# Writing out the sixteen token-group steps of an attention-and-experts kernel, and placing weight preparation, filler products and the hand-over to its second phase anew

## The reference: what is computed

```python
xn = layernorm(x)
x = x + attn(xn) + ffn(xn)
# attn: 16 heads of 8; scores = cov(q, k)/8 + var(q)*var(k)/8, softmax, times v, times Wo
# ffn:  transformer block on xn. Its attention runs over the 32 SEQUENCES (causal),
#       for each of the 256 positions; x1 = xn + that; then layernorm, a router over 8 experts,
#       the top 2 of them: gates * gelu(h @ w1[e]) @ w2[e]; returns x1 + y
```

## Time and profile before

| | |
|---|---|
| runs | 1037.51, 1038.67, 1039.70 us; median 1038.67 |
| profiled execution: time, span | 1042.3 us, 1040.6 us |
| groups, up to the last `causal_pv` | 0 to 337 us |
| lead-in | 337 to 392.5 us |
| expert blocks | 392.5 to 541 us |
| sequence steps | 541 to 1040.6 us |
| busy: PE, DVE, ACT, POOL | 87%, 77%, 66%, 59% of the span |

### The profile page before, as it was taken

The page is one execution under the profiler, slowest core; times in us unless marked ns, Lnnn a source line. Parts: engine busy times, 40 slices in busy tenths (PEclk is TensorE's granted clock), DMA queues, the critical chain, the costliest instruction groups (busy, mean ns, idle before and its releaser), DMA issues.

```text
span 1040.6 us, 34011 instructions
## 1 busy us (share of the span) xinstructions
PE 902.4 (87%) x11962; PEld 564.5 (54%) x11962; DVE 805.8 (77%) x2168; ACT 688.4 (66%) x1395; POOL 619.2 (59%) x886
## 2 busy tenths in 40 slices
PE   3687787888787458999998999999999999999997
PEld 2464554555555325788874555555555555555543
DVE  5878687789888374555566899999999999999880
ACT  3667677778886213443445778778777877787774
POOL 4146475676666662222225777877877777787751
PEclk9678899899999657999997999999999999999998
DMA  6515622122221133777741111111111111111111
GB/s 161 78 32 102 151 67 56 49 68 56 52 64 43 41 112 106 227 224 225 232 139 26 39 44 52 36 49 44 49 39 43 50 37 48 44 49 39 41 47 31
DMA packets 110824, 80.52 MB, mean 77 GB/s; under 512 B 23296, under 2 KB 97920, under 8 KB 110720
## 3 DMA queue, kind: packets, MB, share of 16 engines
q1 hardware_dynamic: 99328, 51.78, 20.3%
q0 software_dynamic: 11392, 27.35, 8.6%
HBM read 44.83 MB, written 33.73 MB: 75 GB/s over the span
## 4 chain that ended last, share of the span: by engine, by line
PE 43%; POOL 19%; issue 14%; DVE 13%; ACT 10%; POOLq 0%; DVEq 0%; DMA 0%; ACTq 0%
PE bank L712 36%; POOL xg L611 4%; POOL stack L523 3%; DVE rowmin L1214 3%; PE bank L751 2%; POOL stack L521 2%; PE bank L1019 2%; POOL rstd L489 2%; POOL sq L501 2%; ACT Vexp L1690 2%; ACT gxb L1718 2%; ACT rows L1733 1%; DVE sprobT L1270 1%; POOL sq L503 1%; POOL token_rows L559 1%
## 5 line engine op out<-in xcount | busy, mean ns | idle before, releaser
L1214 DVE TENSOR_REDUCE rowmin<-bank 128x2 f32<-128x512 f32 x512 | 326.9, 684 | 43.5 <-PE bank L712 43.4
L1646 ACT ACTIVATE prob<-bank 128x512 f32<-128x512 f32 x512 | 290.1, 602 | 81.0 <-PE bank L712 80.6
L712 PE MATMUL bank<-QKT 32*128 32x256 f16 x2048 | 185.0, 277 | 16.1 <-DVE rowmin L1214 12.9
L559 POOL DMA_INDIRECT token_rows<-rows,spots x128 | 127.4, 996 | 40.0 <-issue 31.6
L611 POOL DMA_INDIRECT xg<-expert_out,place x128 | 128.0, 1000 | 33.0 <-POOL spare L607 9.4
L712 PE MATMUL bank<-prob,V 128*25 128x256 f32 x2048 | 137.6, 387 | 0.5 <-ACT prob L1646 0.5
L712 PEld LDWEIGHTS bank<-QKT 32*128 32x128 f16 x2048 | 67.3, 93 | 129.6 <-issue 51.9
L1805 ACT ACTIVATE hmid<-bank,wrow,up_scale 128x512 f32<-128x512 f32 x80 | 58.1, 774 | 88.3 <-PE bank L712 88.3
L631 POOL DMA_DIRECT2D expert_out<-y x40 | 30.2, 755 | 118.7 <-DVE y L1523 111.7
L712 PEld LDWEIGHTS bank<-prob,V 128*25 128x25 f32 x2048 | 50.5, 103 | 52.5 <-issue 27.3
L712 PE MATMUL bank<-wrow,hmid 128*128 128x128 f32 x640 | 78.3, 276 | 0.0
(11 more groups left out here) (227 smaller groups left out, 1918.7 us busy)
## 6 DMA issues: line engine op xcount, KB each, us to landing
xrow<-token_rows SPq DMA_DIRECT2D x40, 258.0 KB, 3.2
wrow<-weight_rows SPq DMA_DIRECT2D x40, 257.0 KB, 3.3
expert_out<-y POOLq DMA_DIRECT2D x40, 256.0 KB, 2.8
token_rows<-xrow SPq DMA_DIRECT2D x16, 258.0 KB
xg<-in_L_attn_x SPq DMA_DIRECT2D x64, 64.0 KB, 2.2
x_in<-in_L_attn_x SPq DMA_DIRECT2D x32, 128.0 KB
out_base<-acc SPq DMA_DIRECT2D x64, 64.0 KB
base_t<-out_base SPq DMA_DIRECT2D x32, 128.0 KB, 2.7
```

Source lines behind the costliest of these rows:

```text
L559: pool.indirect_dma_start(token_rows, bass.IndirectOffsetOnAxis(spots[p][:, j:j + 1], 0), rows[p][:, k, t, :].bitcast(U32), None).then_inc ...
L712: return pe.matmul(o, l, r, start=start, stop=stop, skip_group_check=True)
L1214: dve.tensor_reduce(rowmin[h // 8][:, :, h % TILE_ROWS, h // TILE_ROWS % HALF], row_scores[i % 3][:].rearrange("p (s t) -> p s t", s=ST), ...
L1646: act.activation(prob[:, h % 8].rearrange("p t s -> p (t s)"), col_scores[h % 2][:], ACT.Exp, scale=exp_register).then_inc(s_exp, 1)
```

## The change

`run_groups` writes all steps out. `weight_maximum` goes to DVE's step -1 and `expert_biases` to PE's step 0 ahead of `causal_pv(0)`. `expert_weights` becomes `expert_scales` in step 1 and one call for each expert in steps 2 to 9; SP writes `wts` in step 11. PE gets fillers in steps -2 and -1 and behind the last expert block. Sequence 1's stages move ahead inside steps 15 and 16 on all engines, sequence 0's stack transposes move back to step 16, and both sequences now use the same PSUM bank. POOL's sequence steps get a new order: for b up to 0 `features_low` is done one step sooner; step 0's second pair of gathers goes to step 1; from step 2 on `gather_ready` and the first gather stand ahead of `add_selected`.

```diff
 def run_groups(eng, step):
-    for g in range(-3, 3):
-        step(g, g % 4)
-    with eng.Fori(0, 2) as i:
-        for j in range(4):
-            step(4 * i + j + 3, (j + 3) % 4)
-    for g in range(11, GROUPS + 1):
+    for g in range(-3, GROUPS + 1):
         step(g, g % 4)
...
-            return {0: misc[0], 1: bank[3]}[n] if isinstance(n, int) and n < 2 else misc[1]
+            return misc[0] if isinstance(n, int) and n < 2 else misc[1]
...  POOL, group_step
                 if isinstance(g, int) and g == GROUPS - 2:
                     features_squares(0)
                     features_high(0)
                     features_low(0)
-                if isinstance(g, int) and g == GROUPS - 1:
                     scale_x(1)
                 if ahead:
                     scales(g + 3)
                 if tail:
                     add_x(g, r)
+                    if isinstance(g, int) and g == GROUPS - 1:
+                        features_squares(1)
+                        features_high(1)
+                        features_low(1)
                     scatter(g, p, 0)
...  POOL, step(b, p)
+                early = isinstance(b, int) and b <= 0
+                second = isinstance(b, int) and b == 1
                 if norm:
                     scale_x(b + 3)
+                if second:
+                    gather(1 - p, 1, 0)
+                    gather(1 - p, 1, 1)
+                if cur and not early:
+                    gather_ready(b, p)
+                    gather(p, 0, 0)
+                if second:
+                    gather(p, 0, 1)
                 if prev:
                     add_selected(b - 1, 1 - p)
-                if cur and not first:
-                    gather_ready(b, p)
-                    gather(p, 0, 0)
-                if prep and not first:
+                if prep and not early and not second:
                     features_low(p)
-                if cur and not first:
+                if cur and not early and not second:
                     gather(p, 0, 1)
                 if norm:
                     features_squares(b + 3)
-                if first:
+                if cur and not early:
+                    gather(p, 1, 0)
+                if norm:
+                    features_high(1 - p)
+                if early:
+                    features_low(1 - p)
+                if cur and early:
                     gather_ready(b, p)
                     gather(p, 0, 0)
                     gather(p, 0, 1)
-                if cur:
-                    gather(p, 1, 0)
-                if norm:
-                    features_high(1 - p)
-                if cur:
+                if cur and not early:
                     gather(p, 1, 1)
...  POOL, between groups and experts
             run_groups(pool, group_step)
-            features_squares(1)
-            features_high(1)
             step(-1, 1)
-            features_low(0)
...  PE, group_step (steps -2, -1, 0, 15 and 16)
                     weight_sums()
+                    keep_warm(g, 5)
+                if isinstance(g, int) and g == GROUPS:
+                    pe.wait_ge(s_feat, 2)
+                    stack_transposes(0, 0, 0)
                 if late:
                     router_logits(g - 1)
+                if isinstance(g, int) and g == 0:
+                    expert_biases()
                 if tail:
                     causal_pv(g)
...
                 if isinstance(g, int) and g == GROUPS - 1:
-                    stack_transposes(0, 0, 0)
+                    xn_transposes(1, 1)
+                if isinstance(g, int) and g == -2:
+                    first_warm(14)
+                if isinstance(g, int) and g == -1:
+                    keep_warm(g, 8)
                 if norm:
                     hn_transposes(g + 2)
-                if tail:
+                if isinstance(g, int) and g == -2:
+                    first_warm(4)
+                if tail or isinstance(g, int) and g == -1:
                     keep_warm(g, 4)
                 if norm:
                     causal_q(g + 2)
                 if tail:
                     keep_warm(g, 4)
+                if isinstance(g, int) and g == GROUPS - 1:
+                    project_qk(1, 1)
+                if tail:
                     h2_transposes(g, p)
...
+            def first_warm(times):
+                pe.wait_ge(s_ident, 2)
+                pe.wait_ge(s_zeroed, 1)
+                for i in range(times):
+                    mm(seq_bank[0][:], identh[:], stack[0][:].rearrange("p a s h k -> p (a s h k)")[:, 0:512])
...  PE, behind the last expert block
+                for i in range(4):
+                    mm(row_scores[2][:], onesb[:], causal[:].rearrange("k h t -> k (h t)"))
...  DVE, group_step
                     attention_norms()
+                    weight_maximum()
...  (step 16: half_out(0, 0, 0) moved from ahead of the maxima to behind block_numbers)
+                if isinstance(g, int) and g == 1:
+                    expert_scales()
+                if isinstance(g, int) and 2 <= g < 2 + NE:
+                    expert_weights(g - 2)
                 if head:
                     score_maxima(g + 1, 0)
...
+            def expert_weights(e):
+                dve.tensor_scalar(wts[:, e, 0:FF], w1_sb[:, e], w1_scale[:, 0:1], None, ALU.mult).then_inc(s_dve, 1)
+                dve.wait_ge(s_dve, own.next())
+                dve.scalar_tensor_tensor(out=wts[:, e, FF:2 * FF], in0=w1_sb[:, e], scalar=w1_scale[:, 0:1],
+                                         in1=wts[:, e, 0:FF], op0=ALU.mult, op1=ALU.subtract).then_inc(s_setup, 1)
...  ACT, step 15: normalise_x(1) ahead of merged_rows(15), x_out(1) ahead of normalise_x1(15), features(1) behind it
...  SP, group_step
-                    sp.wait_ge(s_setup, 3)
+                if isinstance(g, int) and g == 3 + NE:
+                    sp.wait_ge(s_setup, 2 + NE)
                     sp.wait_ge(s_dma_w2, 16 * FC)
                     sp.dma_start(weight_rows.rearrange("(e p) c -> p e c", p=P), wts[:].bitcast(U32)).then_inc(s_wput, 16)
```

More of the change, by code:

```diff
@@ L637, in step @@
                 pool.sem_clear(s_pool)
-                first = isinstance(b, int) and b == 0
+                early = isinstance(b, int) and b <= 0
+                second = isinstance(b, int) and b == 1
                 if norm:
                     scale_x(b + 3)
+                if second:
[6 more added lines that the diff above has]
+                    gather(p, 0, 1)
                 if prev:
                     add_selected(b - 1, 1 - p)
-                if cur and not first:
-                    gather_ready(b, p)
-                    gather(p, 0, 0)
-                if prep and not first:
+                if prep and not early and not second:
                     features_low(p)
-                if cur and not first:
+                if cur and not early and not second:
                     gather(p, 0, 1)
@@ L721, in xn_transposes @@
                 if isinstance(n, int) and n == 1:
-                    pe.wait_ge(s_sdiff[3], GROUPS)
+                    pe.wait_ge(s_feat, 1)
                 for st in range(ST):
@@ L963, in group_step @@
                     causal_out(g)
-                    if isinstance(g, int) and g == 0:
-                        expert_biases()
                     keep_warm(g, 4)
@@ L981, in group_step @@
                     project_qk(0, 0)
-                if isinstance(g, int) and g == GROUPS - 1:
-                    xn_transposes(1, 1)
                 if isinstance(g, int) and g == GROUPS:
-                    project_qk(1, 1)
                     for i in range(LEAD):
@@ L994, in keep_warm @@
                     return
+                if isinstance(g, int) and g == -1:
+                    pe.wait_ge(s_masks, 1)
                 for i in range(times):
@@ L1367, in group_step @@
                     x1_statistics(g - 1)
-                if isinstance(g, int) and g == GROUPS:
-                    half_out(0, 0, 0)
                 if tail:
@@ L1380, in group_step @@
                     if isinstance(g, int) and g == 0:
-                        weight_maximum()
                         attention_scales()
@@ L1388, in group_step @@
                     block_numbers()
+                    half_out(0, 0, 0)
                 if late:
@@ L1404, in group_step @@
                     attention_gains()
-                if isinstance(g, int) and g == 1:
-                    expert_weights()
             def group_setup():
@@ L1443, in bias_columns, with expert_scales @@
                                   ALU.add).then_inc(s_setup, 1)
-            def expert_weights():
+            def expert_scales():
                 dve.wait_ge(s_setup, 2)
@@ L1451, in expert_weights @@
                 dve.wait_ge(s_dve, own.next())
-                dve.tensor_scalar(wts[:, :, 0:FF], w1_sb[:], w1_scale[:, 0:1], None, ALU.mult).then_inc(s_dve, 1)
+            def expert_weights(e):
```

(15 more changed lines are left out.)

## The result

The changed kernel takes 1055.58 us (median of 20 runs, 1037.23 to 1084.08), the kernel before 1037.76 (20 runs, 1031.87 to 1041.69): ratio 1.0066, 95% interval 1.0036 to 1.0096. The change made the kernel slower, by 0.7 to 1.7%, where 1002 us was forecast. The profiled run took 1062.07 us, 6.5 above the median; its span is 1060.4.

The account below looks back on a forecast made before the run. A quiet group step was taken as a chain through all engines, none full, with slow-clock stretches and long steps to mend. Nine terms summed to 36.6 us, taking the median from 1038.67 to 1002 us, range 988 to 1018.

Parts of the forecast that it names:

- Term 9: Steady sequence steps: a gather ahead of the add covers POOL's 0.59 us wait; 28 times 0.2, 5.5 us gained.
- Term 5: Group steps 2 and 3: moving the weights' write to step 11 halves the DMA burst that stalls TensorE; 7 us gained.
- The rival "stall stays": Step 3's stall belongs to the first pass over the loop's code or returns in step 11; 1009 us, chance 0.12.
- Term 6: Group loop written out: its turn in step 6 goes, 6.2 us, and its end gives 0.5; 6.7 us gained.
- the slower rival: Written-out group code starves, with a 7.8 us stall in each of eight former loop steps; 1064 us, chance 0.04.
- Terms 2 and 3: Group step 0 without bias products in TensorE's path, 3.7 us; step 1 without the scaling of all experts, 5.2 us.
- Term 1: Stretch up to `causal_pv(0)`: fillers warm TensorE's clock for products on the path; 1.2 us gained.
- Term 4: Eight expert pieces in group steps 2 to 9, some 0.65 us each on DVE; 1 us lost.
- Term 7: Lead-in to the experts: sequence 1's features go before POOL's last scatters, so `scale_x(2)` comes sooner; 3.8 us gained.
- Term 8: End of experts and sequence steps 0 and 1: earlier `features_low` and fillers keeping the clock up; 4.5 us gained.
- The rival of no change: Three to four starving stalls, or group gains eaten by POOL at the last scatters, leave the time unchanged; chance 0.02.

Follow-up runs that it names:

- the spread clears: Changed kernel with the eight transfers clearing the end blocks issued one in each of group steps 2 to 9, not all in step 2: 1043.76 us, ratio 1.0043.
- both mends: Changed kernel with GpSimd's old order from sequence step 2 on and clears one a step in group steps 2 to 9: 1108.89 and 1113.76 us on two chips.

## Why the prediction was wrong

- **Term 9, the steady sequence steps, failed, in sign.** It took POOL's 0.59 us of waiting for idle time to be covered. That wait put the addition at a place where its end lets VectorE's splits through. The text costed the moved addition and gather by the POOL instructions they displace and looked for no one that they displace on VectorE. Measured: 0.6 us more a step (some 18 us) and some 28 us of long steps, -45.5 in place of +5.5. Where the wait keeps the slot, the gain is there: 0.26 us a step against the 0.2 forecast. The forecast did hold the mechanism: the stretched scatter of the earlier trace rows led to it, but it was weighed for the eight pieces alone, which don't meet it (DVE 0.34 and 0.48 us for each piece; steps 4, 6 and 7 at 17.8 to 18.1). The trace before showed it closer by, in the other pair's split of 0.65 us at 621.36. The Trainium skill (SBUF — State Buffer, "SBUF: two separate sides") has DVE and GpSimd exclude each other for whole instructions, whichever starts first; of DVE's instructions it names those in a 2-port mode and, against a GpSimd instruction that reads SBUF, those with two SBUF inputs, as the second split is. The traces agree for that split: 0.18 us becomes 0.75 behind the addition and 1.46 behind the addition and the copies.
- **Term 5 named the wrong burst.** That a load of DMA makes the stall was right, but the clears alone make the 5.14 us. That TensorE's instructions come late behind it isn't shown. 1.9 us came in place of 7.0, and spreading the clears took 7.3 more off the two steps. The rival "stall stays" had the time, though it laid the stall on the first pass over the code.
- **Term 6 was mis-sized.** The turn's 6 us went (step 6 at 18.10), but steps 5, 8 and 10 rose by 1.7, 1.9 and 4.2 over their own windows before (18.34, 17.30 and 17.85). Net 1.4 us with the pieces. (What the text calls step 12 is the window of step 13, and its step 10 is step 11; neither carries a number of the sum beyond 0.5 us.) That is what the slower rival foresaw, at an eighth of the size it needed.
- **Terms 2 and 3** held to 0.2 us. **Term 1** gained 0.6 of 1.2, within its bounds; over the versions of the changed kernel `causal_pv(0)` came at 38.4 to 43.7. **Term 4** cost nothing to be seen, though a piece takes 0.83 us and not 0.65. **Term 7** gave 4.7 against 3.8.
- **Term 8** gave 8.6 up to the first `z_out`, above its bound of 7. The kernel before ran at clock 0.5 from 544.5 us for 10.2 and from 568.4 for 6.8; in the changed kernel the clock is full from 524 to 560. It gave the fillers up to 3 us for this; what of the 8.6 is the clock's no run separates.
- **The sum** of all without term 9 was 31.1 predicted and 25.7 measured. 5.4 us of the miss are theirs, 51 are term 9's. That the smaller terms add up so well is in part luck: terms 5 and 6 missed by 5.1 and 4.3 us (6 with the pieces) and term 8 gave 4.1 too much. With the old order in place of term 9 the change gives 1016.76 us.
- **The chance** of 0.04 for slower stood on starving code alone. No rival asked what POOL's work would meet at its new place. (The rival of no change asks for three to four stalls, where 36.6 / 7.8 is 4.7.)

## What to carry to other kernels

Before moving an instruction on one of two engines that share a port, list what the other engine runs at the new place, and give the short instructions there on which TensorE waits a price of the whole POOL instruction, and of those queued behind it if they may miss the gap (0.75 and 1.46 us here). Look for short instructions that are already stretched in the trace before. An idle gap of the engine may be the slot that these use; where the slot matters, a semaphore can keep it, and here such a wait, with the spread clears, paid 4 to 5%. Test each burst of DMAs by itself: the clears' 2.1 MB in step 2 made step 3 7.3 us longer, the write's 2.1 MB in step 11 did no harm.

## What was not expected of the hardware

The effect of a collision has two levels. In the four profiles with the new order, the whole addition and no added wait, from 600 to 1000 us, none of TensorE's 66 waits for the shifts of up to 0.83 us came with a fall of its clock. Of the 26 of 1.3 us and more 22 did, for 3 to 10 us, and such a step took 2 to 5 us more. Three waits lay between (1.03 to 1.26 us), one of them with a fall. With POOL's instruction halved no wait of the first level was left in this stretch.

Chips differ by 8.5% on the same program (1035 against 1122 to 1127 us), and nearly all of it lies in written-out or long code: group steps of 24 us against 18, the last sequence steps of 21 against 14, while steady sequence steps in their loop, in the old order, are 15.2 and 15.1. Within a group step it lies in TensorE's run of small products, from `causal_pv` up to the transposes `bank<-ident,so_nat`: 11 us on the median with both mends on a slow chip, 5.7 with the old order on the quick one; the rest of the step takes 13.9 against 12.6. Rows of that run in step 5 on the slow chip (11.6 us; 7.6 on the quick one):

```profile
161.93 0.38 PE L718 MATMUL bank<-causal,seq_eye 32*128 32x512 bf16 x1 [1.24 <-issue]
164.03 0.43 PE L718 MATMUL bank<-Kexp,gqT 32*32 32x128 f32 x5 [0.30 <-issue]
165.50 2.14 PE L718 MATMUL bank<-Kexp,gqT 32*32 32x128 f32 x14 [0.28 <-issue]
168.41 1.45 PE L718 MATMUL bank<-Kexp,gqT 32*32 32x128 f32 x54 [0.77 <-issue]
```

The waits for nothing that the profile names add up to 2.9 us here, to 2.5 in the same run on the quick chip. The difference lies inside rows that count as busy, such as the 14 products at 165.50 that take 2.14 us.

This may be a slower supply of instructions; no run settles its cause.
